# Rank scores taken token by row inside the next unit's first product, and x1 turned by two transposing DMAs per tile

## What is computed

```
up, delta = x @ up_w.T, x @ gate_w.T - local_point
a = up @ approx.T + sum over m=1..6 of (sign * |delta|^m / m! * up) @ fuse[m].T
a = a + (silu(x @ ffn_gate.T) * (x @ ffn_up.T)) @ ffn_down.T        # inner width 1248
x1 = layernorm(x + a)
inter = (x1 @ c1.T) @ c2.T                                          # 512 -> 16 -> 1792
idx = argmax over each of the 56 blocks of 32 columns of inter
h = relu(x1 @ w1[idx].T)                                            # one hidden value per block
out = layernorm(x1 + h @ w2t[idx])
```

## Time and profile before

| | us |
|---|---|
| median of 3 runs | 767.73 (767.20 to 769.23) |
| the profiled execution | 767.48 |
| its span, first to last instruction | 765.6 |
| TensorE busy (matmul) | 741.8 (97%) |
| VectorE busy | 488.7 (64%) |
| ScalarE busy | 227.6 (30%) |
| GpSimd busy | 158.1 (21%) |

### The profile page before, as it was taken

One profiled execution on the slowest core, in us unless ns is written; L12 is line 12 of the kernel. 1 busy time (PEld: TensorE's weight loads), 2 busy tenths in 40 slices (PEclk: granted clock), 3 DMA queues, 4 the chain that ended last, 5 costly groups with the idle time before them and its releaser, 6 DMA issues. The chain is left out here.

```text
span 765.6 us, 12508 instructions
## 1 busy us (share of the span) xinstructions
PE 741.8 (97%) x3607; PEld 345.6 (45%) x3607; DVE 488.7 (64%) x883; ACT 227.6 (30%) x356; POOL 158.1 (21%) x132
## 2 busy tenths in 40 slices
PE   6999999999989999999999999999999999999995
PEld 2444444444444444445444444444444444444442
DVE  4887676696867779676867779654765461125115
ACT  1645457435622221222122212321222121222210
POOL 0434442211111111111111112212121212222111
PEclk9999999999999999999999999999999999999998
DMA  8447318410000000000000152004100005001001
GB/s 317 189 137 234 55 24 309 109 55 1 1 2 1 2 1 0 1 1 1 1 2 2 39 103 52 2 1 97 51 5 1 0 12 140 1 0 56 0 0 55
DMA packets 17956, 39.40 MB, mean 51 GB/s; under 512 B 2438, under 2 KB 10246, under 8 KB 17030
## 3 DMA queue, kind: packets, MB, share of 16 engines
q1 hardware_dynamic: 15814, 34.81, 14.4%
q0 software_dynamic: 2112, 4.19, 3.3%
HBM read 34.56 MB, written 4.44 MB: 51 GB/s over the span
## 5 line engine op out<-in xcount | busy, mean ns | idle before, releaser
L414 PE MATMUL acc<-big,work 128*128 128x512 f16 (+1 forms) x1104 | 249.7, 379 | 0.4 <-issue 0.2
L916 POOL TENSOR_TENSOR work<-work 128x512 f32 (+1 forms) x96 | 114.5, 1196 | 521.4 <-ACT work L824 285.4
L402 PE MATMUL pb<-xs,big 128*128 128x512 f16 (+1 forms) x816 | 187.2, 379 | 2.2 <-DVE work L1201 2.1
L402 PE MATMUL pa<-xs,big 128*128 128x512 f16 (+1 forms) x816 | 187.2, 379 | 1.9 <-ACT work L819 1.1
L414 PEld LDWEIGHTS acc<-big,work 128*128 (+1 forms) x1104 | 106.9, 98 | 122.6 <-issue 0.9
L402 PEld LDWEIGHTS pb<-xs,big 128*128 128x128 f16 (+1 forms) x816 | 79.5, 98 | 98.5 <-issue 4.1
L402 PEld LDWEIGHTS pa<-xs,big 128*128 128x128 f16 (+1 forms) x816 | 78.9, 98 | 95.0 <-issue 3.7
L891 ACT ACTIVATE work<-work 128x512 f32 x56 | 35.1, 627 | 227.7 <-DVE work L1416 227.7
L481 PE MATMUL acc<-big 128*128 128x512 f16 x336 | 73.7, 379 | 0.6 <-POOL big L923 0.6
L1416 DVE SCALAR_TENSOR_TENSOR work<-big,const_sb,pa 128x512 f32<-128x512 f16 (+1 forms) x28 | 20.7, 739 | 80.8 <-PE pa L402 80.8
L824 ACT ACTIVATE work<-work 128x512 f32 (+1 forms) x40 | 25.2, 630 | 114.6 <-DVE work L1201 114.6
(11 more groups left out here) (135 smaller groups left out, 579.3 us busy)
## 6 DMA issues: line engine op xcount, KB each, us to landing
big<-in_w_all SPq DMA_DIRECT2D x2, 3840.0 KB, 16.7
big<-spread_rows SPq DMA_DIRECT2D x16, 448.0 KB, 7.1
big<-in_x_t SPq DMA_DIRECT2D x16, 256.0 KB, 4.1
rows<-in_x POOLq DMA_DIRECT2D x4, 1024.0 KB, 9.9
big<-in_w_all SPq DMA_DIRECT2D x2, 1536.0 KB, 9.9
out<-rows SPq DMA_DIRECT2D x3, 1024.0 KB, 4.4
big<-in_w_all SPq DMA_DIRECT2D x1, 2048.0 KB, 15.8
big<-in_w_all SPq DMA_DIRECT2D x2, 1024.0 KB, 5.6
```

The source lines that it names most:

```text
L402: mm = nc.tensor.matmul(dst[:, :], weights(wp)(kc * P, P), x_part16(g, xp, kc), start=(kc == 0 and wp == xp), stop=(kc == KC - 1 and wp == 1))
L414: mm = nc.tensor.matmul(acc[t][:, :], act_part(pair, j, ap, t * P, P), weights(wp)(0, H), start=(first and ap == wp), stop=(last and ap == 1))
L916: nc.gpsimd.tensor_tensor(act_part(pair, j, 1), act32[j], act_part(pair, j, 0), ALU.subtract).then_inc(act_lo, 1)
```

## The change

**TensorE.** `transposes` is gone, with its eight blocks per tile. `z_product` no longer makes z transposed: the turned x1 is the stationary operand and the 16 columns of c1 the moving one, so z comes out with a token per row, by 8 matmuls of 32 or 16 columns into `pick_a`. They stand inside the first gate (or hidden) product of the unit that also scores the tile, behind its third and fourth quarter (`between`). A new `turn_z` behind the unit's `pb` product turns the cut pieces of z (one 128x128 bfloat16 block), and after it the winners. Scores 0 and 1 stand behind the `pa` product of j=1, score 2 behind the `pb` product, score 3 behind the first half of the second product (in phase 2 score 3 moves into the next unit).

**DMA.** SyncE's `turn_x1` issues two transposing DMAs per tile (128x512 float16 each, SBUF to SBUF) when the tile's low half is written, and `x1_arrived` signals TensorE; `x1_high` of the next tile waits for the same signal, since it overwrites the source.

**ScalarE.** `x1t_copy` is gone. **VectorE.** `stack_z`'s four operations on 128 columns become `cut_z`, five small ones on 16 to 48 columns, and one copy of the turned pieces; `copy_turned` follows that copy. The reversed ranks are held 448 wide (`rev_wide`) instead of being read 14 times. In phase 1 all four picks come behind `swiglu` of j=0, the last behind `swiglu` of j=1. In phase 2 a `first_unit` places the fourth pick of the tile before it ahead of the moments, behind `mask_hidden(g, 1)`.

c1 is loaded as 128x64 (32 KB) instead of 128x512 (256 KB), with smaller scaling operations on it.

```diff
+            def turn_x1(i):
+                g, t = i // TPG, i % TPG
+                sp.wait_ge(x1_lo, i + 1)
+                for part in range(2):
+                    at = (g * 2 + part) * KC * GT
+                    dst = xs[:, at:at + KC * GT].rearrange("p (k t) -> p k t", k=KC)[:, :, t * P:(t + 1) * P]
+                    sp.dma_start(dst, x1_part[part], transpose=True).then_inc(x1_turned, 16)
+            def x1_arrived(i):
+                sp.wait_ge(x1_turned, 32 * (i + 1))
+                sp.sem_inc(x1t_ready, 1)
+            def send(i, nxt=True):
+                store_turned(i)
+                if nxt:
+                    turn_x1(i + 1)
+                turned_stored(i)
+                if nxt:
+                    x1_arrived(i + 1)
...
-            for i in range(LAST * TPG - 1):
-                store_turned(i)
+            turn_x1(0)
+            x1_arrived(0)
+            for i in range(LAST * TPG - 3):
+                send(i)
             sp.wait_ge(gate_ready, LAST * C1 + 7)
             load_spread(0)
-            store_turned(LAST * TPG - 1)
+            for i in range(LAST * TPG - 3, LAST * TPG - 1):
+                send(i)
             sp.wait_ge(hid_ready, 1)
             load_spread(1)
-            store_turned(LAST * TPG)
-            store_turned(LAST * TPG + 1)
+            send(LAST * TPG - 1)
+            send(LAST * TPG)
+            send(LAST * TPG + 1, False)
             sp.wait_ge(masked, C2)
             load_spread(2)
             store_rows(0)
-            for i in range(LAST * TPG + 2, SPREAD_TILES):
-                store_turned(i)
+            turn_x1(LAST * TPG + 2)
+            x1_arrived(LAST * TPG + 2)
+            send(LAST * TPG + 2)
...
-            def z_product(tile, g, t, dst, free):
+            def z_product(tile, g, t, dst):
                 def part(at):
-                    if at < TPG // 2:
+                    if at < KC // 2:
                         return
-                    if at == TPG // 2:
-                        pe.wait_ge(score_used, free)
-                        pe.wait_ge(x1t_copied, tile + 1)
-                    for kc in range((at - TPG // 2) * 2, (at - TPG // 2) * 2 + 2):
-                        for wp, xp in ((0, 0), (0, 1), (1, 0)):
...
+                    if at == KC // 2:
+                        pe.wait_ge(score_used, tile * PICKS + 3)
+                        pe.wait_ge(x1t_ready, tile + 2)
+                    for kc in range((at - KC // 2) * 2, (at - KC // 2) * 2 + 2):
+                        for xp in range(2):
+                            n = (2 - xp) * RANK
+                            mm = nc.tensor.matmul(dst[:, 0:n], x_part16(g, xp, kc, t * P, P),
+                                                  c1_parts[:, kc * 2 * RANK:kc * 2 * RANK + n],
+                                                  start=(kc == 0 and xp == 0), stop=(kc == KC - 1 and xp == 1))
+                    if at == KC - 1:
+                        mm.then_inc(z_ready, 1)
...
+            def turn_z(tile, dst):
+                pe.wait_ge(z_cut, tile + 1)
+                nc.tensor.transpose(dst[:, :].bitcast(BF16)[:, 0:P], z_split, ident_bf[:, :])
+                turn_winner(tile, dst)
...
+            def cut_z(tile, src):
+                dve.wait_ge(z_ready, tile + 1)
...
+                step(v.tensor_reduce(z_sum, src[:, 0:2 * RANK].rearrange("p (a r) -> p r a", a=2), axis=AX.X, op=ALU.add))
+                settle()
+                step(v.tensor_copy(pieces(0, 3), wide(z_sum, 3)))
+                settle()
+                step(v.tensor_tensor(z_rest, z_sum, z_split[:, 0:RANK], ALU.subtract))
+                settle()
+                step(v.tensor_copy(pieces(3, 3), wide(z_rest, 3)))
+                settle()
+                v.tensor_tensor(pieces(6, 2), wide(z_rest, 2), pieces(3, 2), ALU.subtract).then_inc(z_cut, 1)
...
             def unit1(g, u, tile, nxt=None):
-                stack_z(tile, pick_b)
-                copy_turned(tile, pick_b)
-                pick(tile, 0, pick_a)
+                cut_z(tile, pick_a)
                 swiglu(g, u, 0)
-                pick(tile, 1, pick_b)
+                stack_z(tile, pick_a)
                 if nxt is not None:
                     x1_low(nxt)
+                pick(tile, 0, pick_a)
+                pick(tile, 1, pick_b)
                 pick(tile, 2, pick_a)
                 swiglu(g, u, 1)
                 pick(tile, 3, pick_b)
...
+            def first_unit(g, tile, phase, signal):
+                settle()
                 mask_hidden(g, 1)
-                normalise((GROUPS - 1, 0)[g], (x1_ready, rows_out)[g])
+                if tile is not None:
+                    pick(tile, 3, pick_b)
+                moments((g - 1) % GROUPS, phase)
+                normalise((g - 1) % GROUPS, signal)
```

More of the change, by code:

```diff
@@ L403, in split_product, with second_product @@
                                               start=(kc == 0 and wp == xp), stop=(kc == KC - 1 and wp == 1))
+                    if between is not None:
+                        between(kc)
                 return mm
-            def second_product(pair, j, weights, first, last, done=None, free=None, between=None):
+            def second_product(pair, j, weights, first, last, done=None, free=None):
                 for t in range(TPG):
@@ L545, in unit1 @@
                         pe.wait_ge(w1_lo, 3 * n + 1)
[L546 removed]
+                    split_product(pa, lambda part: w1_part(s, 0, part), g,
+                                  z_product(tile, *own, pick_a) if tile is not None and j == 0 else None).then_inc(gate_ready, 1)
                     if after_gate is not None and j == 0:
                         after_gate()
[L549 to L552 removed]
+                    if tile is not None and j == 1:
+                        scores(tile, 0, pick_a)
+                        scores(tile, 1, pick_b)
                     if not (start and j == 0):
@@ L568, in down @@
                     slot = (C1 - 1 - j) - (u - 1) * 2 if kind != "last" else 1 - j
-                    if tile is not None and j == (1 if kind == "first" else 0):
-                        transposes(tile, pick_a, tile * PICKS + 3)
                     pe.wait_ge(act_lo, m + 1)
@@ L574, in down @@
                                    done=down_ready if last else None,
-                                   free=(lambda t: added(1, g - 1, t)) if first else None,
-                                   between=z_product(tile, g - 1, u - 1, pick_b, tile * PICKS + 4) if tile is not None and j else None)
+                                   free=(lambda t: added(1, g - 1, t)) if first else None)
+                    if j == 0 and scored is not None:
+                        scores(scored, 3, pick_b)
             def group1(g):
@@ L635, in unit2 @@
                         pe.wait_ge(masked, n - 1)
-                    hidden(dst, u * 2 + j, g)
+                    hidden(dst, u * 2 + j, g, between if j == 0 else None)
                     (after_first, after_hidden)[j]()
@@ L654, in none, with s, zt @@
                 pass
-            def s(tile, k):
+            def s(tile, *picks):
                 def go():
-                    if k >= 2:
-                        pe.wait_ge(score_used, tile * PICKS + (PICKS + k - 1))
-                    scores(tile, k, pick_bank[k % 2])
-                return go
+                    for k in picks:
+                        scores(tile, k, pick_bank[k % 2])
+                return go
+            def zt(tile):
+                return lambda: turn_z(tile, pick_a)
@@ L892, in hidden @@
                     act.activation(act32[j], act32[j], ACT.Relu, scale=HID_SCALE).then_inc(act_hi, 1)
-                    if copy is not None and j == 0:
-                        x1t_copy(GROUPS - 1, copy, pick_a)
                 if high is not None:
```

208 lines of the change are left out of this document (91 added, 117 removed).

## The result

The changed kernel takes 756.75 us (median of 4 runs, 755.62 to 758.11), the kernel before 767.47 in the same comparison: the ratio is 0.9859 [0.9841, 0.9877], 10.7 us or 1.4% faster. Run again beside the first experiments, the same file gave 756.53 and 0.9858 [0.9837, 0.988]. The forecast was 764.3 with a range of 756 to 780: the time lies inside, at its lower end; of the gain, 3.4 us were forecast and 10.7 came.

The account below looks back on a forecast made before the run. TensorE was taken as the bound. Work off TensorE -9.8 and idle -3.1 (together -12.9), `swiglu` waits +2.5 and transposing-DMA waits +7.0 sum to -3.4 us against the median 767.73: 764.3 us, range 756 to 780.

Parts of the forecast that it names:

- the fourth pick 2.5 us into the next unit: VectorE's fourth pick, beside GpSimd, ends 2.5 us into the next unit, hidden in plain units with 3 us to spare.
- `swiglu` is waited for twice: First units of groups 2 and 3: late picks make TensorE wait 1.24 us after tiles 3 and 7, +2.5 us.
- the work on VectorE, ScalarE and the ranks at nothing: VectorE's cut of z and picks hidden in plain units, ScalarE's dropped copy, wide ranks: no change put down.
- D: Time from the end of x1's low half to the transposing DMAs' signal; taken as 4.1 us, between 2.4 and 7.1.
- quick at 2.4: Rival: transposing DMAs take 2.4 us, only tile 12 waits, 0.5 us, both `swiglu` waits stay: 757.8 us; chance 0.20.
- slow: Rival: slow transposing DMAs make z wait at tiles 0, 4, 8, 12, 14; 779.3 us at 7.1; chance 0.24.
- one after the other: Rival: a tile's eight 128x128 blocks pass the DMAs in turn, 10.8 us to the signal: 813.2 us; chance 0.05.
- I take 0.055: Short z product on TensorE priced at 0.055 us, so a tile saves 0.61 us; sixteen tiles -9.8 us.
- its sum, 760.4: Estimate with the Trainium skill's spacing of about 25 ns: a tile saves 0.85 us, term -13.6, time 760.4 us.
- The five covers: Slack before z at tiles 0, 4, 8, 12, 14: 3.0, 3.0, 3.0, 1.9, 4.4 us; waits together +7.0 us.
- Half a gate product, 1.30: Where z products stand in TensorE's gate product: z wanted 1.30 us after its start, used in counting each cover.
- -3.1: TensorE's idle, mostly turns waiting for x1's low half and freed score banks, goes with the turns: -3.1 us.

Follow-up runs that it names:

- experiment 12: Changed kernel with the ranks read narrow again, 32 of them broadcast over the blocks instead of the 448 wide ones: 756.47 us.
- experiment 1: Changed kernel with eight more short products (32 and 16 columns, into unused columns) ahead of each tile's z products: 760.74 us.
- experiment 2: Changed kernel with eight more products of 128 columns, same weight loads, ahead of each tile's z products: 763.0 us.
- experiments 4 and 8: Changed kernel with z products behind the gate product's second and third quarters, 758.15 us; and, in the second run, all eight behind the fourth, 755.49 us.
- experiment 3: Changed kernel without transposing DMAs: TensorE turns x1 and ScalarE copies it, z still by row in its new place: 768.27 us.
- experiment 9: Changed kernel with x1 turned on TensorE and copied by ScalarE, and all eight z products behind the fourth quarter: 765.36 us.
- experiment 5: Changed kernel with a third transposing DMA of 128x512 per tile, issued ahead of the two, into a tensor nobody reads: 764.92 us.
- experiments 6 and 13: Changed kernel with the high half's DMA issued once that half is ready, 752.14 us; in the second run also `swiglu` ahead of the moments, 750.33 us.

## Why the prediction was right or wrong

Right were: TensorE remains the bound; the fourth pick 2.5 us into the next unit (2.4); that `swiglu` is waited for twice (1.24 us each forecast; `pb` starts 1.21 and 1.06 late, of which 1.04 and 0.90 are shown as waits); the work on VectorE, ScalarE and the ranks at nothing (experiment 12); plain tiles hidden. D was right by luck (4.1 forecast, 4.05 measured): I took it from one ordinary load, and it is two issues in a row and a short landing. None of the rivals with another D (quick at 2.4, slow, one after the other) came true. The range held the time.

The size was wrong, mainly by two terms of the sum:

- **"I take 0.055"** for a short product, "since the load and not the columns is then the longer part". It is 0.025 (experiment 1), and 0.055 belongs to 128 columns (experiment 2). That makes 1.10 - 0.20 - 0.055 = 0.845 us saved in a tile for the 0.61 forecast. Group 3 shows 0.86 (17.47 - 16.61); in six units of groups 1 and 2 it is 0.70, as a gap of 0.15 us opens ahead of the second product. Sixteen tiles save 16 x 0.86 - 6 x 0.15 = 12.9, not 9.8: 3.1 of the miss. The Trainium skill (TensorE: Matmul & The Clock Gate, "Wait — 56ns, not 53.3ns?") had about 25 ns for the least spacing; this trace agrees, at 0.025. I gave its sum, 760.4 (760.5 by its own terms), and went by the neighbouring rows, though they differed from the new products in just the size that mattered.
- **The five covers**, +7.0, where 4.2 came. "Half a gate product, 1.30" was a miscount: `part(2)` stands behind the third quarter, 1.94 us in, so each cover was 0.65 too short, 2.6 at the first four tiles (experiments 4 and 8 move z by this much, each way). Tile 12's low half ended at 475.64, 30.3 us into its count, not 31.8, and z was wanted 0.3 sooner: 1.3. Tile 14, for which I had put 1.5, cost nothing: the store did make its DMAs 1.3 us later, but the low half ended at 547.96 and z was wanted at 554.63, a cover of 6.7 us for the 4.4 forecast. Against these stands what no step had: the slow start, 3.0 of the 4.2 us.

Smaller: a third wait for `swiglu`, of 0.74 us, 0.9 in the period of the unit, stands at 445.38 ahead of phase 2, where the same late picks reach a place I had not looked at. And the idle that the change removes was worth more than its **-3.1**: taking the other terms off the 10.24 us that the stretch lost (408.72 to 398.48) leaves 4.8. They are all in the trace of before. The turns started late at five places, 3.3 us, about what I had read as idle. One us more stands behind them in group 3:

```profile
425.60 0.35 PE L534 MATMUL pick_b<-c_stack,big 128*128 128x448 bf16 x1
426.21 0.62 PE L502 MATMUL pick_a<-ident,big 128*128 128x128 f16 x8 [0.26 <-DVE big L1296]
426.98 4.70 PE L414 MATMUL acc<-big,work 128*128 x21
```

From the first of the eight turns to what follows are 0.77 us here for 0.44 elsewhere, three times. The turns themselves start 0.055 apart; it is the `acc` product behind them that comes 0.3 us late, with a `FUSED_REGOPS` of the sequencer in front of it. The last 0.5 are two such gaps behind the turn of the winners, at tiles 0 and 4 (at tile 4 from 310.71 to 311.00, where 0.055 is the rule). I had read the idle time and not the spacing.

The terms as measured: -12.9, -4.8, +2.3 and +0.9 for `swiglu`, +4.2 for z, -10.3; the median fell by 10.7.

As for what the change is made of: with z by row and in its new place alone the kernel stands at 768.3 (experiment 3), with a better place for z at 765.4 (experiment 9). The DMAs are worth 7 us for the turns they take off TensorE, and 3 to 5 more (experiment 9 against 8, experiment 3 against the change) because x1t is then there long before z is due in 12 of 16 tiles.

## What to carry to other kernels

Price a small instruction by a row of its own size, not by the nearest large one; if there is none, run the smallest size by itself. In front of a run of short products, a semaphore must come well ahead (here by about 1.4 us for eight, an estimate), not just in time, and the profile shows no wait when it doesn't: look at the spacing of the products behind it, and at the sequencer's instructions (PEldq) between them. When an edit gives nothing, look at the next wait of the same chain before dropping it: `swiglu` first gave 0.1 us alone, and 1.8 once D was shorter (experiments 6 and 13).

## What the hardware showed that I had not expected

- Short products of 16 and 32 columns behind 128x128 weight loads start 0.025 us apart, though one such load lasts 0.096 us in the profile.
- The same products, behind a semaphore that has only just come, start 0.18 us apart where their addresses depend on two loop counters and 0.12 where they depend on one (experiment 9). The sequencer's `FUSED_REGOPS` in front of each takes 0.103 and 0.046 us there. In a plain unit it is about 2 us ahead, and a wait takes that lead away; without it, at tile 11, nothing is slow. Products of 128 columns behind such a wait are as slow (eight in 1.36 us at tile 0 of experiment 2, for 0.44).
- Issuing a transposing DMA holds SyncE's queue for 1.2 to 1.3 us whether it is 128x512 or 128x1024 (2.0 behind the 1 MB store); landing takes 2.5 and 3.0 us.
- In experiment 5 TensorE's granted clock fell to half for 3.4 us behind one of four waits of 1.2 to 1.6 us, which cost 1.7 us more on one product of 12. That wait cost over twice itself; what decides whether the clock falls no run here shows.
